# Transposed f16 adjacency parts made beside attention heads 3 to 7 instead of in a stage of their own

## The chip, the cores and the metric

The kernel runs on one NeuronCore of one Trainium2 chip. The metric is the device time of one execution in microseconds. Of the kernel before there are three timed runs (3369.71 to 3376.3, median 3375.74) and one profiled execution.

## The reference, cut to what matters

Four layers are computed on x (2048 nodes x 256) with one sparse adjacency matrix `adj` (2048 x 2048, f32). Each reads the layer-normed, rectified x and is added to x.

```
# layer 0: attention, 8 heads over all 2048 nodes
a = einsum('hnd,hmd->hnm', q, k) * scale + adj + adj       # entries with adj == 0 are masked
a = softmax(where(adj == 0, -1e6, a)); a = where(adj == 0, 0, a)
out = einsum('hnm,hmd->hnd', a, v) ... @ Wout
# layer 1: two steps, each with three products of 2048 x 2048 by 2048 x 256
S = adj + I; Rf = S / rowsum(S); Rb = S / colsum(S)[:, None]
Xf = Rf @ Xf; Xb = Rb @ Xb; Xa = nucleus(softmax(Q W2 K^T)) @ Xa
# layers 2 and 3: graph convolutions with adj and with adj + I, scaled by row sums
```

Layers 1 to 3 multiply by `adj` with the nodes on the contraction side, so the kernel keeps a transposed copy of 64·adj in device memory (`adjT_scratch`), as two f16 parts: a rounded one and the rest.

## The kernel before, in words

The kernel is a list of phases, with a barrier of all engines between them: `setup` (loads, layer norm, weights cut into f16 parts), `adjacency`, `attend` (layer 0), then layer 1 twice (`refresh`, `nucleus`), `onward` and `last`. Inside a phase each engine has its own program, in a written order, and waits on semaphores.

`adjacency` takes the 16 row tiles of adj (128 x 2048 f32, 1 MB each) through a ring of four buffers. The first four are loaded during `setup`; ScalarE issues the other loads (L385). Per tile, ScalarE copies it with its columns permuted (L373, which also makes the row sum). VectorE makes the attention bias from it (L405, L409), and SyncE stores the bias (1 MB, L339). TensorE transposes the 16 blocks of 128 x 128 into PSUM (L361), in two halves. For each half ScalarE writes the rounded f16 part (L378), and VectorE sums the columns (L413) and writes the rest part (L415). SyncE stores both parts (1 MB, L341).

`attend` runs 8 heads of 16 items; an item is 128 query rows against all 2048 keys. For item i:

- TensorE makes the logits: `qk`, 24 matmuls of 512 columns, L614, into two PSUM tiles `L` of two banks each.
- VectorE adds the bias and finds the maximum (`peaks`, two L759 of 1024 columns, then L768).
- ScalarE takes the exponential (`exp`: L682, L683) and writes its rounded f16 part e_hi (L688).
- VectorE writes the rest part e_lo (`lo`, L773) and the factors of the row (L776 to L779).
- SyncE's queue transposes both parts with DMA_TRANSPOSE, SBUF to SBUF (L495, L498), and loads the bias of item i+2 (L489).
- TensorE multiplies by V·Wout (`av`, 48 matmuls of 256 columns, L625), and VectorE adds the result to `acc` (`add`, L784).

The order of the engines in the loop of a head (14 turns, t = 0 to 13, with i = 16h + t) is written out: TensorE does qk(i+2), av(i). VectorE does lo(i+1), peaks(i+2), add(i), masks. ScalarE does exp(i+2). SyncE does the bias load and the two transposes of item i. In `exp` the write of e_hi waits for the transpose of the e_hi before it (one buffer), and `lo` for that of the e_lo before it.

At the turn of a head TensorE projects K, Q, V and V·Wout of the next head (`project`, L589 and L571); ScalarE and VectorE write each result bank as two f16 parts (`evacuate`, L695, L793). There are eight banks of PSUM: four in `L`, two `VP`, two `AVB`. The projection of K starts in the two `VP` banks (`EARLY = 2`) and then goes on in the four banks of `L`.

Of the kernel before, what the change touches and what calls it, by code (L numbers as in the profile page):

```python
# [31 lines left out]
ds = bass.ds  # L32

P = 128
# [72 lines left out]
def build(nc, a, out):  # L107
# [8 lines left out]
    with g:  # L116
# [31 lines left out]
        with ExitStack() as c:  # L148
# [4 lines left out]
            with ExitStack() as c1:  # L153
                rows = [sb(c1, f"adj_rows{u}", [P, N]) for u in range(ADJ_AHEAD)]
                phase(setup, a, bias_d, acc, ident, am, winv, sc, halfp, WH, WL, hT_hi, hT_lo, rows, rows_here)
                phase(adjacency, a["adj"], bias_d, at_d, sc, ident, deg, row_mask, rows, rows_here)
            phase(attend, a["L0_gnn_Wout"], bias_d, acc, ident, winv, sc, WH, WL, hT_hi, hT_lo, row_mask,
                  (a, deg, scales, ident16, halfp, gb, x_d, wtop))
# [152 lines left out]
def adjacency(nc, sb, ps, sem, adj, bias_d, at_d, sc, ident, deg, row_mask, A, loaded):  # L311
# [4 lines left out]
    (copied, zeroed, made, dve, tposed, hi_done, lo_done, summed) = (  # L316
        sem("adj_" + s) for s in ("copied", "zeroed", "made", "dve", "tposed", "hi", "lo", "summed"))
    stored = [sem(f"bias_stored{q}") for q in range(2)]
    at_stored = [sem(f"at_stored{q}") for q in range(2)]
    rows = adjacency_rows(adj)  # L320
    AHEAD = ADJ_AHEAD
    HALF = N // 2
    with ExitStack() as c:
        W = [sb(c, f"adj_permuted{q}", [P, N]) for q in range(2)]
        E = sb(c, "adj_zero", [P, N])
        count = sb(c, "adj_count", [P, T])
        B = [sb(c, f"adj_bias{q}", [P, N]) for q in range(2)]
        AT = [sb(c, f"adjT{q}", [P, 2, T, P], F16) for q in range(2)]
        col = sb(c, "col_parts", [P, T, T])
        TP = [ps(c, f"adj_tp{q}", [P, N]) for q in range(2)]  # L330
        FREE = 2
        block = nc.Block()
        with block:
            @block.sync
            def _(sp):
                def store(i, u):
                    n, q, turn = AHEAD * i + u, u % 2, 2 * i + u // 2
                    sp.wait_ge(made, n + 1 + FREE)
                    sp.dma_start(bias_d[ds(n, 1), :, :].rearrange("a p m -> p (a m)"), B[q][:, :]).then_inc(stored[q], 16)  # L339
                    sp.wait_ge(lo_done, 2 * n + 2 + 2 * FREE)  # L340
                    sp.dma_start(at_d[ds(n, 1), :, :].rearrange("a p m -> p (a m)"),  # L341
                                 AT[q][:, :, :, :].rearrange("p x m n -> p (x m n)")).then_inc(at_stored[q], 16)

                with sp.Fori(0, T // AHEAD) as i:
                    for u in range(AHEAD):
                        store(i, u)
                for q in range(2):
                    sp.wait_ge(stored[q], 16 * CH + 16)
                    sp.wait_ge(at_stored[q], 16 * CH + 16)

            @block.tensor
            def _(pe):
                with pe.Fori(0, T // AHEAD) as i:
                    for u in range(AHEAD):
                        n, q = AHEAD * i + u, u % 2
                        pe.wait_ge(loaded[u], 16 * i + 16)
                        rows_u = permuted(A[u][:, :])
                        for h in range(2):
                            pe.wait_ge(lo_done, 2 * n + h + 1)
                            for t in range(T // 2 * h, T // 2 * (h + 1)):  # L360
                                last = nc.tensor.transpose(TP[q][:, t * P:(t + 1) * P], rows_u[:, t // 2, t % 2 * P:(t % 2 + 1) * P], ident[:, :])  # L361
                            last.then_inc(tposed, 1)

            def half(x, h):
                return x[:, T // 2 * h:T // 2 * (h + 1), :].rearrange("p a b -> p (a b)")

            @block.scalar
            def _(s):
                def tile(i, u):
                    n, q, turn = AHEAD * i + u, u % 2, 2 * i + u // 2  # L370
# [4 lines left out]
                    s.wait_ge(at_stored[q], 16 * turn + 16)  # L375
                    for h in range(2):
                        s.wait_ge(tposed, 2 * n + h + 1)
                        nc.scalar.activation(half(AT[q][:, 0, :, :], h), TP[q][:, HALF * h:HALF * (h + 1)], ACT.Copy,  # L378
                                             scale=A_SCALE).then_inc(hi_done, 1)

                with s.Fori(0, T // AHEAD - 1) as i:
                    for u in range(AHEAD):
                        tile(i, u)
                        s.wait_ge(copied, AHEAD * i + u + 1)
                        s.dma_start(A[u][:, :], rows[ds(2 * i + 2 + u // 2, 1), u % 2, :, :].rearrange("a p m -> p (a m)")).then_inc(loaded[u], 16)  # L385
                for u in range(AHEAD):
                    tile(T // AHEAD - 1, u)

            @block.vector
            def _(v):  # L390
                nc.vector.memset(count[:, :], 0.0).then_inc(made, FREE)
                v.wait_ge(made, FREE)
                for q in range(2):
                    nc.vector.memset(count[:, :], 0.0).then_inc(stored[q], 16)
                    v.wait_ge(stored[q], 16)
                    nc.vector.memset(count[:, :], 0.0).then_inc(at_stored[q], 16)
                    v.wait_ge(at_stored[q], 16)
                nc.vector.memset(count[:, :], 0.0).then_inc(lo_done, 2 * FREE)
                v.wait_ge(lo_done, 2 * FREE)
                with v.Fori(0, T // AHEAD) as i:  # L400
                    for u in range(AHEAD):
                        n, q, turn = AHEAD * i + u, u % 2, 2 * i + u // 2
# [4 lines left out]
                        v.wait_ge(stored[q], 16 * turn + 16)  # L407
# [3 lines left out]
                        for h in range(2):  # L411
# [2048 lines left out]
```

## Time and profile before

| | |
|---|---|
| timed runs | 3369.71, 3375.74, 3376.3 us |
| profiled execution, its own time | 3375.48 us |
| its span | 3373.6 us |
| TensorE busy, weight loads | 2892.8 us (86%), 2147.8 us (64%) |
| VectorE, ScalarE busy | 2192.1 us (65%), 1342.0 us (40%) |
| granted TensorE clock, mean | 0.936 |
| DMA | 396.80 MB in 587856 packets, of which 538563 under 512 B |

A busy time is the union of an engine's instructions. Matmuls are pipelined and their ends are modelled, so a TensorE that shows as always busy can still have a little room. What paces a stretch is read from the order in time: which instruction each one starts behind. The span is divided by phases: `setup` up to 58 us, `adjacency` to 199 us, `attend` to about 1912 us, and layers 1 to 3 from there.

### The profile page before, as it was taken

How to read it: one execution, taken by the hardware profiler on the slowest of the kernel's cores; microseconds unless marked ns; L12 is line 12 of the kernel's file. 1: busy time of each engine (PE TensorE's matmuls, PEld its weight loads, DVE VectorE, ACT ScalarE, POOL GpSimd, SP SyncE). 2: the span in 40 equal slices, each digit the busy share in tenths (PEclk: the TensorE clock that was granted, in tenths of full speed). 3: DMA queues.
4: the chain of work that ended last, by engine and by line, in shares of the span. 5: the costliest groups of instructions: out<-in, count | busy, mean ns of one | idle time of the engine just before them, and what ended most of it. 6: DMA issues, size and time to landing. Idle time of an engine off the chain costs nothing. (4 is left out here: it accounts for less than half of the span.)

```text
span 3373.6 us, 55939 instructions
## 1 busy us (share of the span) xinstructions
PE 2892.8 (86%) x20376; PEld 2147.8 (64%) x20376; DVE 2192.1 (65%) x4346; ACT 1342.0 (40%) x1734; POOL 59.8 (2%) x71
## 2 busy tenths in 40 slices
PE   2469999999999999999999778878884669687599
PEld 1356676766767667676676447656553556576488
DVE  7966555565555655556556488788488887895531
ACT  5743434434344343443434322333326364522221
POOL 0000000000000000000000000000000000000110
PEclk7579999999999999999999889998997889899899
DMA  7937848578485784857848413000010010100500
GB/s 288 371 144 178 195 107 199 124 177 196 106 199 124 177 196 105 199 124 177 197 102 210 120 47 98 26 13 26 26 38 26 1 51 2 50 26 1 231 1 26
DMA packets 587856, 396.80 MB, mean 118 GB/s; under 512 B 538563, under 2 KB 553414, under 8 KB 562118
## 3 DMA queue, kind: packets, MB, share of 16 engines
q1 hardware_dynamic: 585990, 382.49, 42.1%
q10 hardware_dynamic: 1728, 12.58, 1.1%
q8 instruction: 72, 1.18, 0.2%
q14 instruction: 66, 0.54, 0.1%
HBM read 223.05 MB, written 37.75 MB: 77 GB/s over the span
## 5 line engine op out<-in xcount | busy, mean ns | idle before, releaser
L773 DVE SCALAR_TENSOR_TENSOR e_lo<-e,e_hi 128x2048 f16<-128x2048 f32 x128 | 293.2, 2291 | 435.3 <-ACT e_hi L688 435.3
L625 PE MATMUL av<-vw_hi,pT_hi 128*128 128x256 f16 x2048 | 559.5, 273 | 8.0 <-DMA pT_lo<-e_lo 8.0
L625 PE MATMUL av<-vw_hi,pT_lo 128*128 128x256 f16 x2048 | 559.4, 273 | 0.0
L625 PE MATMUL av<-vw_lo,pT_hi 128*128 128x256 f16 x2048 | 559.4, 273 | 0.0
L614 PE MATMUL logits<-kT_hi,qT_hi 128*128 128x512 f16 x1024 | 388.6, 379 | 2.8 <-DVE att_small L759 1.9
L614 PE MATMUL logits<-kT_lo,qT_hi 128*128 128x512 f16 x1024 | 388.1, 379 | 0.0
L614 PE MATMUL logits<-kT_hi,qT_lo 128*128 128x512 f16 x1024 | 388.1, 379 | 0.0
L682 ACT ACTIVATE att_small<-att_small,minus 128x1 f32<-128x1 f32 x128 | 37.6, 294 | 784.3 <-DVE att_small L768 784.3
L759 DVE CUSTOM_DVE_ANT_0 e<-logits,bias,att_small 128x1024 f32<-128x1024 f32 x256 | 328.6, 1283 | 0.4 <-issue 0.3
L2000 DVE SCALAR_TENSOR_TENSOR nuc_junk<-nuc_e,nuc_thr 128x2048 bf16<-128x2048 f32 x140 | 323.7, 2348 | 4.3 <-issue 0.4
L683 ACT ACTIVATE e<-e,att_small,sc 128x2048 f32<-128x2048 f32 x128 | 266.2, 2080 | 0.0
L688 ACT ACTIVATE e_hi<-e 128x2048 f16<-128x2048 f32 x128 | 244.5, 1910 | 15.2
L625 PEld LDWEIGHTS av<-vw_hi,pT_hi 128*128 128x128 f16 x2048 | 200.8, 98 | 44.7 <-issue 8.5
L625 PEld LDWEIGHTS av<-vw_lo,pT_hi 128*128 128x128 f16 x2048 | 200.8, 98 | 36.4
L625 PEld LDWEIGHTS av<-vw_hi,pT_lo 128*128 128x128 f16 x2048 | 200.8, 98 | 23.6
L1660 PE MATMUL nuc_l<-logit_k,logit_q 128*128 128x512 f32 x256 | 133.4, 672 | 62.0 <-ACT nuc_e L1855 56.0
L614 PEld LDWEIGHTS logits<-kT_hi,qT_hi 128*128 (+1 forms) x1024 | 100.0, 98 | 123.8 <-issue 15.8
L614 PEld LDWEIGHTS logits<-kT_hi,qT_lo 128*128 (+1 forms) x1024 | 100.2, 98 | 120.8
L614 PEld LDWEIGHTS logits<-kT_lo,qT_hi 128*128 (+1 forms) x1024 | 100.2, 98 | 106.4
L1636 PE MATMUL nuc_l<-nuc_u,nuc_xsT 128*128 128x256 f32 x320 | 92.4, 445 | 80.5 <-ACT nuc_xsT L1833 71.1
L361 PE MATMUL adj_tp<-ident,adj_rows 128*128 128x128 f32 x256 | 59.5, 411 | 91.4 <-DVE adjT L415 61.0
L1660 PEld LDWEIGHTS nuc_l<-logit_k,logit_q 128*128 128x128 f32 x256 | 53.3, 216 | 130.9 <-issue 65.8
(417 smaller groups left out, 5802.6 us busy)
## 6 DMA issues: line engine op xcount, KB each, us to landing
bias<-bias_scratch SPq DMA_DIRECT2D x130, 1024.0 KB, 4.9
bias_scratch<-adj_bias SPq DMA_DIRECT2D x16, 1024.0 KB, 4.5
adjT_scratch<-adjT SPq DMA_DIRECT2D x16, 1024.0 KB, 5.8
nuc_at_hi<-adjT_scratch SPq DMA_DIRECT2D x32, 512.0 KB, 3.8
nuc_at_lo<-adjT_scratch SPq DMA_DIRECT2D x32, 512.0 KB, 4.6
adjT<-adjT_scratch SPq DMA_DIRECT2D x16, 1024.0 KB, 19.8
adj_rows<-in_adj_dram ACTq DMA_DIRECT2D x12, 1024.0 KB, 6.8
adj_rows<-in_adj_dram SPq DMA_DIRECT2D x4, 1024.0 KB, 14.0
```

Of the source, the lines that this page charges most:

```text
L361: last = nc.tensor.transpose(TP[q][:, t * P:(t + 1) * P], rows_u[:, t // 2, t % 2 * P:(t % 2 + 1) * P], ident[:, :])
L614: last = nc.tensor.matmul(o, QT[w][:, k, ds(t * P, P)], KT[x][:, k, c0:c0 + BANK], start=(k == 0 and w == x == 0), stop=(k == 1 and w == 1))
L625: last = nc.tensor.matmul(AV[par], PT[par][w][:, m, :], VW[x][:, m, :], start=(m == 0 and w == x == 0), stop=(m == T - 1 and w == 1))
L682: nc.scalar.activation(masked(par), nb(par), ACT.Exp, bias=minus[:, 0:1], scale=1.0)
L683: nc.scalar.activation(E[par][:, :], E[par][:, :], ACT.Exp, bias=nb(par), scale=sc[:, 0:1], accum_out=ssum(par)).then_inc(exped, 1)
L688: nc.scalar.activation(EH[:, :], E[par][:, :], ACT.Copy, scale=P_SCALE).then_inc(hi_s, 1)
L759: return nc.vector.tensor_tensor_reduce(E[par][:, cols], L[half][:, :], B[par][:, cols], 1.0, (small[:, par, 6:7], m0(par))[half], ALU.add ...
L773: nc.vector.scalar_tensor_tensor(out=EL[:, :], in0=E[par][:, :], scalar=P_SCALE, in1=EH[:, :], op0=ALU.mult, op1=ALU.subtract).then_inc(lo ...
L1636: nc.tensor.matmul(WEIGHTED, xT[:, n * D + k * P:n * D + (k + 1) * P], U[:, n, k, :], start=(n == k == 0), stop=False)
L1660: last = nc.tensor.matmul(scores_in(i)[:, b * BANK:(b + 1) * BANK], QT[:, i * P:(i + 1) * P], KT[:, b * BANK:(b + 1) * BANK], start=True, ...
L2000: nc.vector.scalar_tensor_tensor(out=void[:, k % 2, :], in0=e[:, g % 2, k, 0:N], scalar=bound[:, k:k + 1], in1=e[:, g % 2, k, 0:N], op0=co ...
```

## The change

In `adjacency` the transposes, both f16 parts, their stores and the column sums by VectorE go. TensorE instead adds up the columns with a row of ones (64 f32 matmuls of 512 columns into one partition of PSUM), ScalarE copies the sums (one instruction over 1 x 2048), and 16 small matmuls turn them into columns. ScalarE issues the load that refills a buffer once its own copy and TensorE's sums have read it.

The transposed parts are made in `attend`, beside heads 3 to 7. The adjacency is read again from its input, in 64 pieces of 128 rows x 512 columns (256 KB). Heads 3 to 7 have 14 slots each, 70 in all, one per item of the loop; in slot s the engines do, with every step skipped where the piece doesn't exist:

- SyncE: first the four stores of piece s-3 (64 KB each, in runs of 128 f16 values), then item's bias load and two transposes, then the two DMA transposes of piece s-2 (128 x 512 each), then the load of piece s.
- ScalarE: after exp(i+2), the rounded part of piece s-1 (`piece_top`), read with its columns permuted.
- VectorE: after lo(i+1), peaks(i+2), add(i), masks (and, in head 7, shift), the rest part of piece s-1 (`piece_rest`), once ScalarE has made the top.

The pieces lie in columns of h^T that heads 0 to 3 have used up. The loops of heads 3 to 7 are written out on SyncE, ScalarE and VectorE. The projection of K goes over eight banks. In head 0 ScalarE evacuates V·Wout ahead of exp(0), and VectorE looks for the weights' maxima ahead of peaks(0).

```diff
 def adjacency(...)                                      # TensorE
+                    for b in range(N // BANK):
+                        cols = slice(b * BANK, (b + 1) * BANK)
+                        last = nc.tensor.matmul(CS[0:1, cols], ones[:, 0:1], A[n % AHEAD][:, cols], start=n == 0, stop=n == T - 1)
+                    last.then_inc(summed, 1)
...
                         s.wait_ge(copied, AHEAD * i + u + 1)
+                        s.wait_ge(summed, AHEAD * i + u + 1)
                         s.dma_start(A[u][:, :], rows[...]).then_inc(loaded[u], 16)
...
 def attend(...)
-        EARLY = 2
+        K_BANKS = (VP[0], VP[1], bank[2], bank[3], bank[0], bank[1], AVB[0], AVB[1])
...
+                def piece_load(n):                       # SyncE
+                    if n >= 2:
+                        sp.wait_ge(piece_lo, n - 1)
+                    sp.dma_start(PA[n % 2], piece_rows[tile // 2, tile % 2, part, :, :]).then_inc(piece_here[n % 2], 16)
+                def piece_turns(n):
+                    n -= 2
+                    sp.wait_ge(piece_lo, n + 1)
+                    if n:
+                        sp.wait_ge(piece_stored, 64 * n)
+                    for x in range(2):
+                        sp.dma_start_transpose(PX_T[x], PX[x]).then_inc(piece_turned, 16)
+                def piece_stores(n):
+                    n -= 3
+                    sp.wait_ge(piece_turned, 32 * n + 32)
+                    for x in range(2):
+                        for q in range(2):
+                            sp.dma_start(piece_out[tile, part % 2, :, x, :, q, part // 2, :],
+                                         PX_T[x][q * HALF:(q + 1) * HALF, :, :]).then_inc(piece_stored, 16)
+                def items_and_pieces(h):
+                    for t in range(T):
+                        piece_stores(slots(h, t))
+                        item(T * h + t, (t + 2) % T, t % 2)
+                        piece_turns(slots(h, t))
+                        piece_load(slots(h, t))
...
+                def piece_top(n):                        # ScalarE
+                    n -= 1
+                    s.wait_ge(piece_here[n % 2], 16 * (n // 2) + 16)
+                    if n:
+                        s.wait_ge(piece_turned, 32 * n)
+                    nc.scalar.activation(PX[0].rearrange("p (c r) -> p c r", c=CH), permuted(PA[n % 2]), ACT.Copy,
+                                         scale=A_SCALE).then_inc(piece_hi, 1)
+                def items_and_pieces(h):
+                    for t in range(SLOTS):
+                        exp(T * h + t + 2, t % 2)
+                        piece_top(slots(h, t))
...
+                def piece_rest(n):                       # VectorE
+                    n -= 1
+                    v.wait_ge(piece_hi, n + 1)
+                    nc.vector.scalar_tensor_tensor(out=PX[1].rearrange("p (c r) -> p c r", c=CH), in0=permuted(PA[n % 2]), scalar=A_SCALE,
+                                                   in1=PX[0].rearrange("p (c r) -> p c r", c=CH), op0=ALU.mult, op1=ALU.subtract).then_inc(piece_lo, 1)
+                def items_and_pieces(h):
+                    for t in range(SLOTS):
+                        item(h, t, t % 2, link)          # lo(i+1), peaks(i+2), add(i), masks
+                        if h == HEADS - 1:
+                            shift(T * h + t, t, t % 2)
+                        piece_rest(slots(h, t))
```

## Rows read from the trace of the kernel before

**Rows 1.** Windows: busy us and count per engine, granted clock, DMA share, GB/s

```profile
core 0: us, PE busy (x) PEld busy (x) DVE busy (x) ACT busy (x) POOL busy (x), PEclk, DMA share, GB/s
64.00:164.00 100.00, 46.82 (x202) 37.78 (x200) 97.58 (x85) 71.03 (x50) 0.00 (x0) 0.59 0.98 373
205.00:1860.00 1655.00, 1639.44 (x11967) 1165.46 (x11966) 964.86 (x1908) 683.31 (x759) 8.19 (x3) 1.00 0.66 160
```

**Rows 2.** Timelines of VectorE and ScalarE over one item: start, duration, [idle before]

```profile
912.38 2.29 DVE L773 SCALAR_TENSOR_TENSOR e_lo<-e,e_hi 128x2048 f16<-128x2048 f32 x1 [3.94 <-ACT e_hi L688]
915.29 1.28 DVE L759 CUSTOM_DVE_ANT_0 e<-logits,bias,att_small 128x1024 f32<-128x1024 f32 x1
918.11 0.21 DVE L768 TENSOR_SCALAR att_small<-att_small,sc 128x1 f32<-128x1 f32 x1
918.36 0.29 ACT L682 ACTIVATE att_small<-att_small,minus 128x1 f32<-128x1 f32 x1 [6.12 <-DVE att_small L768]
920.85 1.91 ACT L688 ACTIVATE e_hi<-e 128x2048 f16<-128x2048 f32 x1
922.91 2.29 DVE L773 SCALAR_TENSOR_TENSOR e_lo<-e,e_hi 128x2048 f16<-128x2048 f32 x1 [3.91 <-ACT e_hi L688]
```

**Rows 3.** Timeline of TensorE: the first logits matmul of two items

```profile
927.85 0.38 PE L614 MATMUL logits<-kT_hi,qT_hi 128*128 128x512 f16 x1
938.27 0.38 PE L614 MATMUL logits<-kT_hi,qT_hi 128*128 128x512 f16 x1
```

**Rows 4.** Instruction groups: what copies and rests of this shape took

```profile
L373 ACT ACTIVATE adj_permuted<-adj_rows x16: 3913/3944/4097, 58.2 to 175.3; 128x2048 f32<-128x2048 f32 x16
L706 ACT ACTIVATE wo_hi<-wo_stage,winv x8: 705/706/722, 203.2 to 1682.1; 128x512 f16<-128x512 f32 x8
L805 DVE SCALAR_TENSOR_TENSOR wo_lo<-wo_stage,winv,wo_hi x8: 750/751/753, 204.0 to 1682.9; 128x512 f16<-128x512 f32 x8
```

**Rows 5.** Timeline of SyncE's queue over one item: issue start and length

```profile
912.35 1.72 SPq L495 DMA_TRANSPOSE pT_hi<-e_hi  x1
914.77 2.17 SPq L498 DMA_TRANSPOSE pT_lo<-e_lo  x1
918.27 0.33 SPq L489 DMA_DIRECT2D bias<-bias_scratch  x1
922.87 1.92 SPq L495 DMA_TRANSPOSE pT_hi<-e_hi  x1
1761.09 1.05 SPq L515 DMA_DIRECT2D x_scratch<-wo_stage  x1
```

**Rows 6.** DMA: one item, a transposing microsecond, a bias microsecond; packets and issues

```profile
912.35:922.87 10.52, 10.52 (x76) 7.14 (x74) 6.28 (x13) 4.28 (x4) 0.00 (x0) 1.00 0.84 199
916.00:917.00 1.00, 1.00 (x12) 0.89 (x10) 0.88 (x4) 0.00 (x0) 0.00 (x0) 1.00 1.17 224
910.00:911.00 1.00, 1.00 (x6) 0.49 (x5) 0.00 (x0) 0.87 (x3) 0.00 (x0) 1.00 1.02 434
DMA packets 4317, 2.10 MB, mean 191 GB/s; under 512 B 4189, under 2 KB 4189, under 8 KB 4189
pT_lo<-e_lo SPq DMA_TRANSPOSE x128, 4.3
```

**Rows 7.** Adjacency: VectorE's groups, the last stores, a later f32 matmul

```profile
L405 DVE TENSOR_SCALAR adj_zero<-adj_permuted x16: 1212/1216/1228, 62.5 to 185.9; 128x2048 f32<-128x2048 f32 x16
L409 DVE SCALAR_TENSOR_TENSOR adj_bias<-adj_permuted,sc,adj_zero x16: 2351/2352/2353, 63.9 to 187.2; 128x2048 f32<-128x2048 f32 x16
194.29 0.33 SPq L341 DMA_DIRECT2D adjT_scratch<-adjT  x1
199.23 0.39 SPq L537 DMA_DIRECT2D wo_stage<-in_L_gnn_Wout_dram  x1
bias_scratch<-adj_bias SPq DMA_DIRECT2D x16, 1024.0 KB, 4.5
2841.31 3.70 PE L1660 MATMUL nuc_l<-logit_k,logit_q 128*128 128x512 f32 x8
```

**Rows 8.** Waits of TensorE, 205 to 1860 us: total, times, longest

```profile
PE logits L589 <- DVE kT_lo L793: 9.4, 7, 1.4
PE vw_ps L571 <- DVE vw_lo L793: 3.4, 1, 3.4
```

More of the change, by code:

```diff
@@ L326, in adjacency @@
         count = sb(c, "adj_count", [P, T])
+        ones = sb(c, "adj_ones", [P, 1])
         B = [sb(c, f"adj_bias{q}", [P, N]) for q in range(2)]
[L328 to L330 removed]
+        col = sb(c, "col_sums", [1, N])
+        CS = ps(c, "col_sums_ps", [P, N])
+        CT = ps(c, "col_sums_turned", [P, BANK])
         FREE = 2
@@ L351, in _ @@
             @block.tensor
             def _(pe):
[L353 to L362, printed above, removed]
@@ L367, in _ @@
+                pe.wait_ge(row_here, 1)
+                for t in range(T):
+                    last = nc.tensor.matmul(CT[:, t:t + 1], permuted(col[0:1, :])[:, t // 2, t % 2 * P:(t % 2 + 1) * P], ones[0:1, 0:1],
+                                            start=True, stop=True)
+                last.then_inc(turned, 1)
             @block.scalar
@@ L395, in _ @@
                     v.wait_ge(stored[q], 16)
[L396 to L402, printed above, removed]
+                with v.Fori(0, T // 2) as i:
+                    for q in range(2):
+                        n = 2 * i + q
                         v.wait_ge(copied, n + 1)
@@ L470, in attend, with piece, slots @@
         AV = [AVB[n][:, 0:D] for n in range(2)]
-        EARLY = 2
+        bank = [L[b // 2][:, b % 2 * BANK:(b % 2 + 1) * BANK] for b in range(4)]
         VW_RING = (VP[0], VP[1], AVB[0])
+        K_BANKS = (VP[0], VP[1], bank[2], bank[3], bank[0], bank[1], AVB[0], AVB[1])
         GAMMA_BETA_READ = 9
-        bank = [L[b // 2][:, b % 2 * BANK:(b % 2 + 1) * BANK] for b in range(4)]
         kinds = [(1, KT), (0, QT), (2, VT), None]
+        done_h = [[hT[:, k, 0:(FIRST_HEAD + 1) * ROWS] for k in range(KC)] for hT in (hT_hi, hT_lo)]
+        PA = [done_h[0][k].bitcast(F32) for k in range(KC)]
+        PX = [done_h[1][0][:, x * BANK:(x + 1) * BANK] for x in range(2)]
+        PX_T = [done_h[1][1][:, x * BANK:(x + 1) * BANK].rearrange("p (b n) -> p b n", n=P) for x in range(2)]
+        def piece(n):
+            tile, part = n // PARTS, n % PARTS
+            return tile, part
+        def slots(h, t):
+            return SLOTS * (h - FIRST_HEAD) + t if isinstance(h, int) and h >= FIRST_HEAD and t < SLOTS else None
         def m0(par): return small[:, par, 0:1]
@@ L708, in begin @@
                         evacuate(h, n)
-                    exp(T * h, 0)
-                    evacuate(h, 3)
+                    if isinstance(h, int) and h == 0:
+                        evacuate(h, 3)
+                        exp(T * h, 0)
+                    else:
+                        exp(T * h, 0)
+                        evacuate(h, 3)
                     exp(T * h + 1, 1)
@@ L902, in _ @@
                     masks(2, 0, link)
-                link = items(HEADS - 1, ends=True)
+                with v.Fori(0, FIRST_HEAD) as h:
+                    turn_of_heads(h, items(h))
+                for h in range(FIRST_HEAD, HEADS - 1):
+                    turn_of_heads(h, items_and_pieces(h))
+                link = items_and_pieces(HEADS - 1)
                 lo(T * HEADS - 1, 1, link)
```

141 lines of the change are left out of this document (80 added, 61 removed).

## The prediction

> **What bounds the kernel now.** I read the windows by stage first. In the adjacency stage VectorE is busy 97.58 of 100 us and the DMA engines show a share of 0.98 at 373 GB/s [rows 1]: two limits at once. In the attention stage TensorE is busy 1639 of 1655 us at full clock, and VectorE and ScalarE only 58% and 41% [rows 1]. Read alone, this says that VectorE and ScalarE have time to spare there. So I read next, in time order, what starts behind what over one item of a head [rows 2]. The reader is to see one closed chain:
>
> - VectorE's e_lo starts at 912.38, the moment e_hi is there; the logits' maxima follow without a gap (first half at 915.29), and the factor of L768 starts at 918.11.
> - ScalarE starts at 918.36, ends e_hi at 920.85 + 1.91 = 922.76, and VectorE's next e_lo starts at 922.91.
>
> Nobody outside of the chain is waited for. VectorE's idle 3.94 us is ScalarE's part of it, ScalarE's idle 6.12 us is VectorE's. The chain takes 922.91 - 912.38 = 10.53 us per item. TensorE's own work takes 938.27 - 927.85 = 10.42 us per item [rows 3]. So two loops run with nearly the same period, and in neither engine of the chain is the idle time free: whatever stands inside it lengthens the item, whatever stands beside it does not.
>
> **The pieces, beside heads 3 to 7.** In slot t ScalarE runs exp(i+2) and then `piece_top`. VectorE runs lo(i+1), peaks(i+2), add(i), masks, and then `piece_rest`, which waits for the top of the same slot, so for the whole of exp(i+2). Behind the waiting instruction in VectorE's queue stands lo(i+2), which before started right at e_hi(i+2). Everything the piece costs on both engines is therefore put into the chain between e_hi and e_lo:
>
> - `piece_top`, 128 x 512 f32 read with permuted columns (a step of 8 values). The same permuted copy of four times the size took 3944 ns, while the contiguous e_hi of that size took 1.91 us [rows 2, 4]. A contiguous 128 x 512 copy took 706 ns [rows 4]. With a fixed part of about 0.3 us (from 0.706 and 1.91 us on a straight line), the permuted one is 0.3 + (3.94 - 0.3)/4 = 1.2 us. Bounds: 0.7 (contiguous) and 1.35 us.
> - `piece_rest`, the same shape on VectorE: 0.75 us contiguous [rows 4]. No permuted read by VectorE is in the trace. I take 0.75, because the nearest row is of the same operation and size. Upper bound: 0.75 x 3.94/1.91 = 1.5 us.
> - One more handover between the engines, 922.91 - 922.76 = 0.15 us [rows 2].
>
> Sum 2.1 us, bounds 1.55 and 3.0. The item of a slot becomes 10.53 + 2.1 = 12.6 us. There are 64 pieces in 64 slots: 64 x 2.1 = **+134 us** (99 to 192). TensorE then idles 12.6 - 10.4 = 2.2 us per item. The trace has whole attention windows at clock 1.00 only with TensorE nearly full; I take 1.00 also here and put its fall into the upper part of the range.
>
> The Trainium skill's page "SBUF — State Buffer", section "Door 1: The DMA port swizzle", says that an SBUF access leaves full bandwidth once successive reads fall into new 16-byte lines, that is at a step above 4 f32 values. ScalarE's 3944 ns agree with it. By this rule VectorE's permuted read would be slowed too, which is the third rival below.
>
> **The DMA queue in a slot.** An item moves two transposes and one bias load. A transposing microsecond moves 224 GB/s at a share of 1.17, a bias microsecond 434 GB/s [rows 6]. So the 1 MB of the transposes takes 4.8 us and the 1 MB of the bias 2.4 us, with start-up gaps a share of 0.84 [rows 6]. A piece adds transposes of 0.25 MB (1.2 us), a load of 0.25 MB (0.6 us), and 0.25 MB of stores in 1024 runs of 256 B. No store of such runs is in the trace. The transposes' packets are 256 B too (1.05 MB in 4096 of the 4189 small ones), so I take their rate, 1.2 us; bounds 0.6 (the bias rate) and 2.6 us (twice the transposes' time). Together 4.8 + 2.4 + 1.2 + 0.6 + 1.2 = 10.2 us, which fits in 12.6 but would hardly have fitted in 10.5.
>
> SyncE's queue is in order, so I followed it, from e_hi at 0. The transpose of e_hi is issued at 0.1. The e_lo transpose is issued at 4.5 (e_lo is 2.1 late), its issue takes 2.2 and it lands 4.3 later [rows 5, 6]. The piece's transposes are issued behind it, about 0.5 us each, and land at 10.0. The load's issue may take 1.05 us, as the store behind a transpose did [rows 5]. The stores wait for that landing: issued from 10.05 to 11.4, and the bias load behind them at 11.4 instead of right behind the maxima. The next e_hi transpose comes at 12.7 and finds the bias still moving, up to 15. It ends near 17.4, before the e_lo transpose would start at 18.3. So the next e_lo is not late, and av(i), which needs it, runs from 11.6 while both have landed by 8.9. Cost 0, thanks to the chain having grown. The margin is about 1 us; what it costs without it is rival 2.
>
> The Trainium skill's page "DMA: Bandwidth & Descriptors", section "Specifications", asks for at least 512 B per run for line rate and calls smaller ones read-modify-write. The stores here are 256 B; no run of before shows such a store.
>
> **The adjacency stage.** Of VectorE's 8.2 us per tile (15 steps from 63.9 to 187.2) there remain L405 and L409, 1.22 + 2.35 + about 0.35 = 3.9 us [rows 7]. ScalarE keeps the copy, 3.94 + 0.2, and an issue, about 4.6 us. TensorE's four f32 matmuls per tile take 4 x 0.44 = 1.8 us at full clock (3.70 us for eight [rows 7]) and twice that at half clock; both lie below ScalarE. The new wait for `summed` holds only ScalarE's reload behind it, and TensorE is ahead. DMA: before, 12 loads and 32 stores of 1.05 MB; now 12 and 16, 29.4 MB. At 373 to 380 GB/s this is 78 us, above ScalarE's 16 x 4.6 = 74. From the first reload at 63.0 it ends at 141, and 3 us go on the last landing: 144. Before, the last store was issued at 194.3 and the next phase issued at 199.2 [rows 7]; the last of the new stores lands where I put 144 to 146. The column sums' tail (copy of 1 x 2048 about 2 us, 16 small matmuls about 2) lies beside the last bias (2.35 us and 4.5 us to land [rows 7]). Saved: **-53 us** (bounds -40, if the DMA falls to 320 GB/s in so mixed a traffic, and -58, if ScalarE sets the pace).
>
> **The turn of heads and head 0.** K over eight banks takes away the wait for the first K rest, 9.4 us in 7 turns [rows 8]. In the three turns before the pieces it is gone: -4. In the four turns beside pieces the K evacuation starts 2 us later and the gain is used up by it: 0 (-5 to +7). In head 0 TensorE's 3.4 us wait goes: **-3** (0 to -3.4). Layers 1 to 3 read the same bytes from the same place: 0.
>
> **Sum.** The profiled execution's own time 3375.5 (span 3373.6 and 1.9 around it; the median is 3375.7, so nothing is to be shifted): 3375.5 - 53 - 4 - 3 + 134 = 3449.5. I predict 3448 us. About 0.2% (7 us) can be told from no change.
>
> **Rivals.**
>
> 1. Faster: the pieces are free, because they fit in VectorE's 3.9 and ScalarE's 6.1 us of idle time per item. For it: the busy shares of 58% and 41%. Against it: these gaps wait for each other and for nothing else. It decides if e_lo doesn't have to follow e_hi at once, from a slack of 2.1 us per item. Then 3375.5 - 53 - 9 - 3 = 3310 us.
> 2. The DMA queue sets the item. If each 256 B store costs 2.6 us or its four issues take 0.9 us each (one took 1.05 behind a transpose), the loop from stores over bias, e_hi, e_lo and piece transposes back to the stores is 0.7 + 3.6 + 2.7 + 4.8 + 1.2 + 0.6 = 13.6 us, with a slow bias start 14. Then 64 x (13.9 - 10.5) = 218: 3375.5 - 60 + 218 = 3533 us.
> 3. VectorE's permuted read is slowed as ScalarE's is. For it: ScalarE's 3.94 against 1.91 us [rows 2, 4]. Against it: nothing measured. The rest then takes 1.35 to 1.5 us: + 64 x 0.6 to 0.75, so 3490 us.
> 4. The pieces come out at half their price, since the DVE and ScalarE parts overlap in their pipelines or TensorE's loop had been the longer one in the first half of a head: 64 x 1.1: 3386 us.
>
> Chances: forecast 0.53, rival 1 0.09, rival 2 0.13, rival 3 0.18, rival 4 0.07. Range 3396 to 3520: it holds the forecast with its bounds, rival 3, and the lower part of rival 2, and leaves out rival 1, most of rival 4 and the rest of rival 2. Faster 0.11 (rival 1, and a little of rival 4), within 0.2% 0.03, slower 0.86.
>
> **What the profile after would show.** The e_lo group has a start to start of 12.6 us in slots against 10.5 in heads 0 to 2; `piece_top` near 1.2 us, `piece_rest` near 0.75; between e_hi and e_lo about 2.2 us instead of 0.15; ScalarE's idle before L682 still near 6, now ended by the same L768; TensorE with a gap of 2 us per item; the first item of attention starting near 147 instead of 202. If the e_lo instructions stay 10.5 us apart, rival 1 holds. If ScalarE waits for `hi_turned` or TensorE for pT_lo, it is rival 2. The forecast fails altogether if the order of `piece_rest` and the next `lo` turns out not to bind.

## The result and the profile after

| | median us | runs | ratio to before, 95% interval |
|---|---|---|---|
| before | 3372.72 | 3365.39 to 3376.3 (4) | |
| after | 3788.04 | 3781.08 to 3792.01 (4) | 1.1231, 1.1207 to 1.1254 |

The change makes the kernel 415 us slower. The prediction was 3448 us with a range to 3520: the sign was right, the size of the loss was not. The profiled execution took 3786.7 us (span 3784.9).

First where the time went. The three lines are VectorE's e_lo instructions (count, duration min/median/max in ns, first to last start in us) in before, in after, and in the first experiment, which has no pieces:

```profile
L773 DVE SCALAR_TENSOR_TENSOR e_lo<-e,e_hi x128: 2279/2292/2294, 258.6 to 1894.1; 128x2048 f16<-128x2048 f32 x128
```

```profile
L839 DVE SCALAR_TENSOR_TENSOR e_lo<-e,e_hi x128: 2276/2286/2295, 208.9 to 2312.6; 128x2048 f16<-128x2048 f32 x128
```

```profile
L845 DVE SCALAR_TENSOR_TENSOR e_lo<-e,e_hi x128: 2280/2292/2293, 214.6 to 1832.2; 128x2048 f16<-128x2048 f32 x128
```

The first e_lo comes 258.6 - 208.9 = 49.7 us earlier. Most of it is the adjacency stage: attention's first load is issued at 152.04 for 199.23 [rows 7], 47.2 us earlier, where 53 were forecast. From the first e_lo to the last it takes 2103.7 us for 1635.5, +468. Behind the last one are 3784.9 - 2312.6 = 1472.3 us for 1479.5, -7. Sum -49.7 + 468.2 - 7.2 = +411, the difference of the two spans. The loss lies in the heads with pieces alone: from the first e_lo of head 0 to that of head 3 it takes 627.1 us for 629.0, from there to the last e_lo 1476.6 for 1006.5.

The windows of after, to be read against [rows 1]: VectorE falls from 97.58 to 63.88 us and the DMA share from 0.98 to 0.85 in the adjacency stage; in attention TensorE is idle 244 of 1655 us and its granted clock is 0.92 for 1.00. Over this window no engine is near full, and the DMA engines' share is 0.65 (0.70 in items with pieces, see run 16).

```profile
core 0: us, PE busy (x) PEld busy (x) DVE busy (x) ACT busy (x) POOL busy (x), PEclk, DMA share, GB/s
64.00:164.00 100.00, 76.60 (x235) 26.59 (x233) 63.88 (x79) 66.36 (x38) 4.00 (x2) 0.86 0.85 326
205.00:1860.00 1655.00, 1410.79 (x9613) 977.79 (x9612) 811.11 (x1577) 597.97 (x653) 0.00 (x0) 0.92 0.65 150
```

So one item has to be read in order of time, as [rows 2] and [rows 5] were. SyncE's queue in one slot of after (issue start and length), then ScalarE, then VectorE (start, duration, [idle before]):

```profile
1303.76 0.60 SPq L487 DMA_DIRECT2D bias<-bias_scratch  x1
1304.50 5.45 SPq L493 DMA_TRANSPOSE pT_hi<-e_hi  x1
1310.07 1.87 SPq L496 DMA_TRANSPOSE pT_lo<-e_lo  x1
1316.14 2.50 SPq L516 DMA_TRANSPOSE hT_lo<-hT_lo  x2
1318.69 0.57 SPq L506 DMA_DIRECT2D hT_hi<-in_adj_dram  x1
1319.86 2.58 SPq L526 DMA_DIRECT2D adjT_scratch<-hT_lo  x4
1322.48 0.61 SPq L487 DMA_DIRECT2D bias<-bias_scratch  x1
1323.23 5.41 SPq L493 DMA_TRANSPOSE pT_hi<-e_hi  x1
```

```profile
1312.07 1.91 ACT L732 ACTIVATE e_hi<-e 128x2048 f16<-128x2048 f32 x1 [6.63 <-DMA pT_hi<-e_hi]
1313.89 1.11 ACT L773 ACTIVATE hT_lo<-hT_hi 128x512 f16<-128x512 f32 x1
1321.81 0.30 ACT L726 ACTIVATE att_small<-att_small,minus 128x1 f32<-128x1 f32 x1 [6.82 <-DVE att_small L834]
1330.87 1.91 ACT L732 ACTIVATE e_hi<-e 128x2048 f16<-128x2048 f32 x1 [6.67 <-DMA pT_hi<-e_hi]
```

```profile
1315.03 1.08 DVE L929 SCALAR_TENSOR_TENSOR hT_lo<-hT_hi,hT_lo 128x512 f16<-128x512 f32 x1 [10.70 <-ACT hT_lo L773]
1316.02 2.29 DVE L839 SCALAR_TENSOR_TENSOR e_lo<-e,e_hi 128x2048 f16<-128x2048 f32 x1
```

The item takes 1330.87 - 1312.07 = 18.80 us for 10.53, and it is one loop that now runs through SyncE's queue. From e_hi's start: e_hi to the top 1.82 us, top to rest 1.14, rest to the issue of the piece's transposes 1.11; then SyncE alone: transposes 2.55, load with the wait for the transposes' landing 1.17, four stores 2.62, bias load 0.75; and at 1323.23 the transpose of the e_hi that was written at 1312.07. It was ready 9.2 us earlier (at 1312.07 + 1.91). It takes 5.4 us to issue, and ScalarE's next e_hi starts 7.64 us behind its start. Sum 1.82 + 1.14 + 1.11 + 2.55 + 1.17 + 2.62 + 0.75 + 7.64 = 18.80. The next item's exponential was ready at 1324.1 already; ScalarE then waits for the transpose to land, because there is one buffer for e_hi.

The same in the waits of after (engine, line, what for: total us, times, longest), SyncE's own among them:

```profile
DVE hT_lo L929 <- ACT hT_lo L773: 651.5, 64, 11.9
ACT e_hi L732 <- DMA pT_hi<-e_hi: 374.9, 60, 7.0
PE av L670 <- DMA pT_lo<-e_lo: 339.6, 57, 7.9
SPq L516 <- DVE hT_lo L929: 259.6, 60, 7.6
```

The first line tempts: VectorE waits 651 us for `piece_top`. But the top is a late link of the loop, not its price; the price is in what stands between e_hi and its transpose.

### The profile page after: what moved, and what is told of

It reads as the page before. It is cut to its first block and busy times, and to the rows that moved or that the text cites. A ratio compares the mean times of both kernels' runs of the same rounds, so it can differ in the third digit from the quotient of the medians.

```text
span 3784.9 us, 54717 instructions
## 1 busy us (share of the span) xinstructions
PE 3028.1 (80%) x20280; PEld 2174.1 (57%) x20280; DVE 2173.5 (57%) x4344; ACT 1380.7 (36%) x1767; POOL 57.8 (2%) x71
## 5 line engine op out<-in xcount | busy, mean ns | idle before, releaser
L670 PE MATMUL av<-vw_hi,pT_hi 128*128 128x256 f16 x2048 | 615.5, 301 | 339.6 <-DMA pT_lo<-e_lo 339.6
L670 PE MATMUL av<-vw_lo,pT_hi 128*128 128x256 f16 x2048 | 614.8, 300 | 0.0
L670 PE MATMUL av<-vw_hi,pT_lo 128*128 128x256 f16 x2048 | 612.4, 299 | 0.0
L670 PEld LDWEIGHTS av<-vw_hi,pT_hi 128*128 128x128 f16 x2048 | 219.8, 107 | 415.7 <-issue 365.9
L929 DVE SCALAR_TENSOR_TENSOR hT_lo<-hT_hi,hT_lo 128x512 f16<-128x512 f32 x64 | 69.0, 1078 | 651.5 <-ACT hT_lo L773 651.5
L732 ACT ACTIVATE e_hi<-e 128x2048 f16<-128x2048 f32 x128 | 244.7, 1912 | 381.3 <-DMA pT_hi<-e_hi 374.9
L670 PEld LDWEIGHTS av<-vw_lo,pT_hi 128*128 128x128 f16 x2048 | 219.1, 107 | 49.2
L670 PEld LDWEIGHTS av<-vw_hi,pT_lo 128*128 128x128 f16 x2048 | 220.5, 108 | 45.0
```

Of the source, the lines that this page charges most:

```text
L670: last = nc.tensor.matmul(AV[par], PT[par][w][:, m, :], VW[x][:, m, :], start=(m == 0 and w == x == 0), stop=(m == T - 1 and w == 1))
L732: nc.scalar.activation(EH[:, :], E[par][:, :], ACT.Copy, scale=P_SCALE).then_inc(hi_s, 1)
L929: nc.vector.scalar_tensor_tensor(out=PX[1].rearrange("p (c r) -> p c r", c=CH), in0=permuted(PA[n % 2]), scalar=A_SCALE, in1=PX[0].rearran ...
```

## The experiments

"Slot" is the time of an item with a piece. "Issue" of a DMA is the time that it holds SyncE's queue, and "landing" the moment when its data are there. All times are medians; the kernel before ran beside each set (3370.2 to 3374.3 us).

**1. No pieces.** `PIECES = 0`; the scratch gets the same 16 MB in sixteen 1 MB stores of weights, so the transposed adjacency is missing from it.

```diff
-    PIECES = T * PARTS
+    PIECES = 0
+                        sp.dma_start(at_d[n // 4, :, :], WH[0][...]).then_inc(filled, 16)     # n % 4 == 0
```

> The kernel after with no pieces at all: no loads, tops, rests, transposes or stores of pieces; the transposed parts are not made (16 stores of 1 MB of weights, one in every fourth item of heads 3 to 6, fill the scratch instead). All that is left of the change is the shorter adjacency stage, K over eight banks and the order in head 0. Theory A (SyncE's in-order queue closes a loop through the pieces) and theory B (the DMA engines are full of the 256 B stores) both expect the terms of the prediction without the pieces: 3375 - 53 - 9 - 3 = 3310 us, 3306 to 3325. A third theory, that something else in the change costs (the loops written out, the layers behind), expects 3340 us or more.

3308.39 us, ratio 0.9809 (0.9793 to 0.9826). The sum of all terms but the pieces' was right: in the prediction it was 3375.5 - 60 = 3315. The pieces cost 3788.0 - 3308.4 = 480 us, forecast 134.

The sum, 62 us less than the kernel before where 60 were forecast, is right partly by luck. In this run's trace the first e_lo comes at 214.6, 44 us earlier than before, so the first part saved less than forecast. And from the first e_lo of head 3 to the last it takes 991.0 us, for 1001.7 in run 17, which has the same turn of heads and no pieces either, but loops that are not written out. These 11 us stand in no term of the prediction; they fit the written-out loops (or another order of waits in them), which no run tried alone.

**2. Loads, tops and rests only** (transposes and stores of pieces out, fills in).

```diff
 def piece_turns(n):
+    return
 def piece_stores(n):
+    return
```

> Pieces are loaded, and ScalarE's top and VectorE's rest are made where the change has them; no transposes and no stores of pieces (the parts in the scratch are those of e1). This is the term of +134 us in the prediction by itself. After it, the top takes 1.11 and the rest 1.08 us in the trace of the changed kernel, so the chain should be 10.53 + 1.11 + 1.08 + 0.15 = 12.9 us per slot: e1 + 64 x 2.3 = e1 + 150 us, about 3460. Both theories expect this. If VectorE and ScalarE had time to spare after all, it is e1 + 0 to 30.

3474.98 us: +166.6, 2.6 us a slot. SyncE's wait before the load (for the rest of two pieces earlier, 252.4 us in all) already puts load, bias and pT_hi's transpose behind the next e_hi, and the long issue is here already. So this run is not the chain's +134 alone:

```profile
1396.88 0.33 SPq L507 DMA_DIRECT2D hT_hi<-in_adj_dram  x1
1397.26 0.43 SPq L488 DMA_DIRECT2D bias<-bias_scratch  x1
1397.81 5.06 SPq L494 DMA_TRANSPOSE pT_hi<-e_hi  x1
```

**3. Everything but the stores.**

> As the change, but without the stores of the pieces (their place in the scratch is filled as in e1); loads, tops, rests and the pieces' transposes stand where they were. Theory A: SyncE still waits in slot s for a rest that comes only behind the NEXT e_hi, then issues 2.5 us of transposes, 0.6 of load, 0.6 of bias before that e_hi's transpose. Loop: 0.15 + 1.1 + 1.1 + 2.5 + 0.6 + 0.6 + landing 5 to 6 + 1.9 = 13 to 14 us, e1 + 64 x 3.0 = e1 + 160 to 220. Theory B: without the stores the DMA engines are no limit, and it equals e2.

3644.53 us: +169.6 over run 2, 2.65 us a slot, which is the issue of the two transposes (2.50 us and a gap). The last step, the stores, gives 3788.0 - 3644.5 = 143.5, 2.24 us a slot, for an issue of 2.58, against which run 3 has a quarter of a fill a slot (0.43/4 us). Both of the expected sizes were wrong: in this order, every issue on SyncE counts nearly in full.

**4. Another order on SyncE:** bias, pT_hi, the piece's transposes (one slot later), pT_lo, load, stores.

```diff
-                        piece_stores(slots(h, t))
-                        item(T * h + t, (t + 2) % T, t % 2)
-                        piece_turns(slots(h, t))
-                        piece_load(slots(h, t))
+                        item(..., between=lambda: piece_turns(s_ - 1))      # between pT_hi and pT_lo
+                        piece_load(s_ - 1)
+                        piece_stores(s_)
```

> All work of the change, but SyncE's order moved: in a slot it issues bias, transpose of e_hi, the two transposes of a piece whose rest is due by then (one slot later than in the change), transpose of e_lo, load, stores. Tops and rests stay in the chain. Theory A: the wait for a rest behind the next e_hi is gone, SyncE's issues add up to 10.3 us, and the slot falls from 18.8 to 13 to 14.5 us: 3450 to 3580 us. Theory B (the DMA engines need 18 us for a slot's bytes): within 30 us of the changed kernel, 3760 or more.

3534.33 us, ratio 1.048 (1.0459 to 1.0502): 254 us come back with the same work. SyncE's wait for the rest is gone (259.6 us before, 0.3 us here), and its queue is now full, with no pause:

```profile
1397.54 5.31 SPq L493 DMA_TRANSPOSE pT_hi<-e_hi  x1
1402.95 2.51 SPq L517 DMA_TRANSPOSE hT_lo<-hT_lo  x2
1405.58 1.46 SPq L497 DMA_TRANSPOSE pT_lo<-e_lo  x1
1407.10 1.31 SPq L507 DMA_DIRECT2D hT_hi<-in_adj_dram  x1
1408.45 2.58 SPq L527 DMA_DIRECT2D adjT_scratch<-hT_lo  x4
1411.08 0.61 SPq L487 DMA_DIRECT2D bias<-bias_scratch  x1
1411.83 5.39 SPq L493 DMA_TRANSPOSE pT_hi<-e_hi  x1
```

The slot of 1411.83 - 1397.54 = 14.3 us is the sum of its issues, 13.8 us, and the gaps between them.

**5. `piece_top` ahead of `exp`**, one line moved.

> One line moved: ScalarE makes the top of a piece before exp(i+2), in the time in which it waits for VectorE, instead of behind it. So the rest no longer stands between e_hi and e_lo, and it is made before the next e_hi, where SyncE asks for it. All work of the change is done. Theory A (loop and issue time of SyncE's queue): the loop through the rest opens, and what is left is the sum of SyncE's issues in a slot, as in e4: 1.9 + 2.5 + 0.6 + 0.6 + 2.6 + 0.6 + 5.3 = 14.1 us against 10.3: e1 + 64 x 3.8 to 4.5, 3550 to 3600. The theory that only VectorE's and ScalarE's 2.3 us count: changed kernel - 150 = 3640.

3564.51 us, ratio 1.0557 (1.054 to 1.0575). The rest is there when SyncE asks for it: its wait falls from 259.6 to 9.0 us in all, and the item (e_hi at 1397.63 and 1412.42) takes 14.8 us, near the sum of SyncE's issues as in run 4.

**6. Stores in runs of 1 KB** instead of 256 B: another order of the blocks in the scratch, and later stages take them in it.

```diff
-    piece_out = at_d.rearrange("t (h r) (x b a q n) -> t h r x b a q n", ...)
+    piece_out = at_d.rearrange("t (h r) (x a q b n) -> t h r x b a q n", ...)
```

> Only the layout of the scratch changes: the four blocks of a piece lie side by side, so a store moves runs of 1 KB instead of 256 B (64 runs per store instead of 256), and the consumers index the blocks in the new order. Theory A: a store's issue falls from 0.62 to 0.35 us (-1.1 per slot), and the bias load and e_hi's transpose behind it start earlier by the time that the 1024 small runs needed, 3 to 4 us in the trace of the change: 18.8 to about 14 us, 3788 - 64 x 4.5 = 3500, range 3480 to 3620. If the runs' size is without effect on the DMA engines: -64 x 1.1, 3718.

3788.96 us, ratio 1.1235 (1.1216 to 1.1253): no difference, with 684903 packets for 734055. Both expected sizes fell. The four stores' issue is hardly shorter (2.38 us for 2.58), so the queue has as much to issue as before, and what the wider runs save on the DMA engines is hidden.

**7. Piece loads and stores issued by GpSimd.**

> The loads and the stores of the pieces are issued by GpSimd, which is idle, instead of SyncE; SyncE keeps bias, transposes of e and of pieces in the change's order, and with it the wait for a rest behind the next e_hi. Same bytes, same small runs. Theory A: it is e3 without the load's issue on SyncE: 3590 to 3660. Theory B (the 256 B stores fill the DMA engines): the stores are still there, so no gain: 3750 or more.

3674.85 us, ratio 1.0893 (1.0875 to 1.0912): 113 us less, and 15 us above theory A's range. SyncE still waits 271.3 us for the rest.

**8. Runs 5, 6 and 7 together, the piece's transposes behind the next bias load.**

> All repairs together: top before exp, runs of 1 KB, loads and stores of pieces issued by GpSimd, and on SyncE the piece's transposes behind the next item's bias load, so the bias is not directly ahead of e_hi's transpose. SyncE's issues sum to 0.4 + 2.5 + 1.9 + 2.0 = 6.8 us per slot, the DMA engines' bytes to 9.8 us, both below 10.5. Theory A: all is hidden, e1 + 0 to 60, 3310 to 3370, below the kernel before. If DMAs issued by GpSimd or the traffic as such delay the transposes: 3400 or more.

3412.11 us, ratio 1.0109 (1.0092 to 1.0126). This missed the expected range: 104 us over run 1 are left.

**9. The bias load issued by ScalarE**, behind its e_hi, and nothing else.

```diff
 # SyncE, item
-                    sp.wait_ge(logits_read, 2 * i + 2 + READS_FREE)
-                    bias(after, par)
 # ScalarE, exp
                     nc.scalar.activation(EH[:, :], E[par][:, :], ACT.Copy, scale=P_SCALE).then_inc(hi_s, 1)
+                    s.dma_start(B[par][:, :], bias_d[ds(after, 1), :, :]...).then_inc(bias_par[par], 16)
```

> The change as it is, but each bias load is issued by ScalarE, right behind its e_hi write, and no longer by SyncE directly ahead of pT_hi's transpose. Theory A (a transposing DMA that stands directly behind a load in SyncE's queue holds SyncE until that load has landed: its issue takes 5.4 us for 1.9): the slot loses 0.6 us of the bias issue and 3 to 3.5 us of pT_hi's issue, 64 times: 3790 less 230 to 265 us, 3525 to 3560. Theory B (the long issue comes of the DMA engines being shared with the bias load, whoever issues it): the issue stays near 5 us, 3740 to 3790. Theory C (the piece loads and stores behind it in the queue fill the gap): stores now stand directly ahead of pT_hi, and its issue stays above 4 us, 3680 to 3750.

3582.58 us, ratio 1.063 (1.0612 to 1.0648): 205 us less, 3.2 a slot, 23 us above theory A's range and far from the two others. pT_hi's transpose, now behind four stores and not behind the bias load, is issued in 2.0 us:

```profile
1396.99 2.58 SPq L526 DMA_DIRECT2D adjT_scratch<-hT_lo  x4
1399.69 1.96 SPq L493 DMA_TRANSPOSE pT_hi<-e_hi  x1
```

The run moved the load to another queue and to another time at once. ScalarE issues it at 1404.25, and the next transpose of e_hi comes at 1414.89, when the load (median landing 5.3 us) is there. So it shows that the load just ahead was the cause, but it does not decide between theories A and B, because the load was no longer moving. Sorted by this, the transposes of e_hi from 900 us on took 1.96 us (median of 58) where the load had landed and 3.35 us (median of 17) where it was still moving, though in ScalarE's queue; directly behind the load in SyncE's queue they take 5.3.

**10. Run 8's early top, wide stores and GpSimd, with the bias load on ScalarE.**

> SyncE issues transposes only: loads and stores of the pieces are issued by GpSimd, bias loads by ScalarE behind its e_hi write, and piece_top comes before the exp that waits for pT_hi. Theory A (the loss is SyncE's serial issue and its waits): SyncE's sum per slot is 2.5 + 1.9 + 1.9 = 6.3 us for about 12 us of a slot, all hidden; 3308 (the run without pieces) to 3350 us. Theory B (the DMA queues' own time: the extra transposing moves, 0.5 MB a slot at 200 GB/s, 2.5 us, in a row with the tiles' own): 2 to 3 us a slot stay, 3430 to 3500.

3435.62 us, ratio 1.0187 (1.017 to 1.0204). Theory A fell, and the time is in theory B's range. In the slots of head 5 SyncE issues for 8.1 us of 12.5, and the slot stays near 12. Before the piece's transposes SyncE waits for the landing of the stores, 180.6 us in all.

**11. Early top, and loads and stores by GpSimd; SyncE in the change's order.**

> The change with its piece loads and stores issued by GpSimd and piece_top ahead of the exp; SyncE keeps piece transposes, bias, pT_hi, pT_lo in the change's order. Theory A: SyncE issues 2.5 + 0.6 + 5.4 + 1.9 = 10.4 us a slot, and the loop from the rest of a piece to its transposes no longer passes the exp: 3320 to 3420 us. Theory B (early top does not help once the stores have left SyncE; the loop stays e_hi write, rest, turns, bias, pT_hi): near the 3675 us that the queue move alone gave, 3600 to 3680.

3409.77 us, ratio 1.0112 (1.0095 to 1.0129). The slot is the sum of SyncE's issues, 2.50 + 0.57 + 5.09 + 3.15 and gaps, 11.8 us (piece transposes to piece transposes, 1421.67 - 1409.87). The issue of pT_lo is longer here than in after (3.15 us for 1.87), so an issue is not a fixed price:

```profile
1409.87 2.50 SPq L516 DMA_TRANSPOSE hT_lo<-hT_lo  x2
1412.42 0.57 SPq L487 DMA_DIRECT2D bias<-bias_scratch  x1
1413.13 5.09 SPq L493 DMA_TRANSPOSE pT_hi<-e_hi  x1
1418.34 3.15 SPq L496 DMA_TRANSPOSE pT_lo<-e_lo  x1
1421.67 2.50 SPq L516 DMA_TRANSPOSE hT_lo<-hT_lo  x2
```

**12. Early top and bias on ScalarE, the rest as in the change.**

> piece_top ahead of the exp and bias loads issued by ScalarE; loads and stores of the pieces stay with SyncE. Theory A: the two savings add where they take different parts of the loop: the early top gave 224 us and the bias 230 to 265 us of 412 above the kernel before; SyncE's sum is 2.5 + 0.6 + 2.6 + 1.9 + 1.9 = 9.5 us, below a slot of 11.7, so what is left is small: 3320 to 3400 us. Theory B (the issue of pT_hi stays long with four stores directly ahead of it): SyncE's sum is 13 us a slot, 3400 to 3480.

3537.64 us, ratio 1.05 (1.0483 to 1.0518), a miss, and only 27 us below run 5. With the long issue gone SyncE comes early to the stores and stands before them until the piece's transposes have landed, 193.1 us in all for 33.6 in run 5. Early top and bias on ScalarE shorten the same loop and hardly add.

**13, 14. Halves with semaphores of their own** on runs 8 and 10 (a half's transpose waits only for that half's two stores). These runs have 256 B stores again, which runs 8 and 10 had not: two differences at once.

```diff
                     for x in range(2):
+                        if n:
+                            sp.wait_ge(piece_stored[x], 32 * n)
-                        sp.dma_start_transpose(PX_T[x], PX[x]).then_inc(piece_turned, 16)
+                        sp.dma_start_transpose(PX_T[x], PX[x]).then_inc(piece_turned[x], 16)
```

> Piece loads and stores issued by GpSimd, piece_top ahead of the exp, a piece's transposes behind the next bias load, and each half of a piece with semaphores of its own: the transpose of a half waits for that half's two stores alone, and the stores for that half's transpose alone. Theory A (the loop through the turned buffer: transposes issued and landed 5.2 us, stores issued and landed 6.9 us, 12.2 us a slot, set e8_pool_all's 3412): the loop of one half is about 4 + 1 + 4 + 1.3 us = 10.5, below the item's own 10.5 to 11, so 3310 to 3360. Theory B (the DMA engines are the bound, 0.95 of 12.3 us = 11.7 us of work a slot): at least 3308 + 64 x 0.8 = 3360, and hardly below e8: 3370 to 3415.

> The same split halves with bias loads issued by ScalarE, transposes alone with SyncE. Theory A: e10_act_bias_all's loop of 11.9 us and more falls to about 10.5: 3310 to 3360. Theory B (DMA engines at 0.94 busy): 3390 to 3436, as e10.

3411.67 us (1.0118, 1.0095 to 1.0141) and 3437.19 us (1.0208, 1.0176 to 1.0241): as runs 8 and 10, and within theory B's range or 1 us above it.

**15. Run 13 with stores in runs of 1 KB.**

> e13_split_order with its stores in runs of 1 KB for 256 B (layout of the scratch and the order in which later stages take its tiles changed with it). Theory A (packets of 256 B fill the DMA engines, which are now the bound, as they were not when e6_wide_runs changed nothing): 50,000 packets fewer, 3350 to 3390 us. Theory B (the store's packets are no more than a small part of what fills them): 3405 to 3415, as e13.

3388.57 us, ratio 1.0044 (1.0027 to 1.006). Against run 13 the wide runs give 23.1 us; against run 8, which has wide runs and whole-piece semaphores, the split gives 23.5 us. Run 13 alone reads as if the split changed nothing, and so I first read it; it had lost as much by its narrow runs. The fourth combination, narrow runs and no split in this order, was not run.

**16. Run 13 without the stores** (fills as in run 1).

> e13_split_order without the 256 piece stores; the same 16 MB go to the scratch as sixteen fills of 1 MB from weights (so the transposed adjacency is not in it). Loads, tops, rests and piece transposes stay. Theory A (the DMA engines are full and the stores' packets are a part of it): the slot falls to the item's own, 3310 to 3345 us. Theory B (the piece transposes fill them, or hold up the tiles' own transposes whatever is stored): 3380 to 3412.

3328.05 us, ratio 0.9874 (0.9852 to 0.9896). Of the 103 us that run 13 stands over run 1, 84 are the stores and the loop through them; 20 us are left for loads, tops, rests and transposes.

How full are the DMA engines? A window has to be cut by items: with a turn of heads in it, where they have less to do, the share comes out lower. So here are the same eight items (from the sixth e_hi of head 5 to the fourteenth) of run 1, after, run 13, run 15 and run 16:

```profile
1311.11:1392.30 81.19, 81.19 (x567) 55.28 (x566) 48.93 (x102) 34.27 (x33) 0.00 (x0) 1.00 0.93 233
```

```profile
1532.67:1681.34 148.67, 102.38 (x576) 64.12 (x576) 57.17 (x112) 42.41 (x40) 0.00 (x0) 0.82 0.70 155
```

```profile
1351.95:1450.84 98.89, 88.23 (x581) 57.81 (x579) 57.19 (x112) 42.70 (x41) 24.47 (x40) 0.97 1.16 233
```

```profile
1340.78:1435.80 95.02, 85.47 (x582) 56.31 (x581) 56.74 (x112) 43.19 (x41) 22.05 (x41) 1.00 1.16 244
```

```profile
1318.92:1405.51 86.59, 84.85 (x581) 56.44 (x579) 57.24 (x112) 42.81 (x40) 4.29 (x8) 1.00 1.11 267
```

Item times share gives the DMA work of an item: 10.15 x 0.93 = 9.4 us in run 1, 18.6 x 0.70 = 13.0 in after, 12.4 x 1.16 = 14.3 in run 13, 10.8 x 1.11 = 12.0 in run 16. A piece thus adds 3.6 us (after) to 4.9 us (run 13) to the work of run 1's item. A share of 1 is no limit of this measure (it reaches 1.16 here, and 1.17 in [rows 6]), but in run 13 it is as high as anywhere, at 233 GB/s where a bias load alone moved 434 [rows 6].

With SyncE relieved (run 10), the limit is therefore on the DMA side. Two things can make it: the work as such, or the loop of a piece (transposes landed, stores landed, next transposes), in which each landing is late while others move. Run 15 shortened the work and gained 23 us; run 16 took away work and loop at once. They are not told apart.

**17. K over eight banks alone**, on the kernel before (with head 0's new order), five rounds.

> The kernel before with K over eight banks, and head 0's order of exp and V W_o evacuation as in the change; adjacency stage and attention queues as before. Theory A (the run without pieces, 62 us below the kernel before, is the sum of 50 us of the adjacency stage and some 12 us of this part): 3355 to 3365 us. Theory B (the 12 us came of the removed adjacency work, for instance of its later loads, and K's banks gain nothing): 3368 to 3373.

3364.48 us (3360.43 to 3367.39), ratio 0.9974 (0.9963 to 0.9984). This is the only complete kernel here that is faster than the one before, by 8.1 us or 0.24%; the prediction had given these edits 7.

## Why the prediction was off

- **Adjacency stage** (-53 forecast): 47.2 us in after; by the first e_lo, which includes head 0's new order, 49.7 in after and 44.0 in run 1. **Turn of heads and head 0** (-7): 8.1 us in run 17. **Layers 1 to 3** (0): -7 us in the spans of after and before, within the spread of the kernel before (3365.39 to 3376.3). These steps held in kind, with the adjacency stage 6 to 12 us too high; run 1's sum agrees because heads 3 to 7 gave 11 us that no term had.
- **`piece_top`** (1.2 us): 1.11. **`piece_rest`** (0.75, with rival 3 at 1.35 to 1.5): 1.08. VectorE's permuted read is slowed, though less than rival 3 says. As in the Trainium skill's "SBUF — State Buffer", Door 1, the trace agrees that a step of 8 f32 values costs bandwidth on VectorE too. This explains 0.33 x 64 = 21 us of the 346 by which the pieces were under-priced.
- **The failed step** is the DMA queue in a slot, "Cost 0, thanks to the chain having grown". It says that "the piece's transposes are issued behind" the e_lo transpose, at about 7 us behind e_hi, and takes the piece's rest as there. But these transposes are of piece s-2, whose rest VectorE makes in its slot s-1, behind ScalarE's exp and top of that slot, so behind e_hi(i+1). SyncE takes its queue in order: at its wait for that rest (259.6 us, 60 times) it stops, and the transposes, the load, the stores and the bias load all come between e_hi(i+1) and its own transpose. I followed the queue, but did not write down which slot makes the thing each wait asks for. Run 4 shows it: the same instructions in another order, -254 us. The sign that the prediction gave for rival 2 is there: ScalarE waits for e_hi's transpose (374.9 us), TensorE for pT_lo (339.6 us).
- **Mis-sized terms of the same step:** the piece's transposes 0.5 us each to issue (1.26 measured), the four stores 1.35 us in all (2.58), and the transpose of e_hi, which finds the bias still moving, 4.7 us from issue to landing (12.7 to 17.4; 7.6 us measured, 5.4 of them in the issue). Taking the bias load away from there is worth 3.2 us a slot (run 9). Rival 2 had the right kind, an item set by the queue, but a loop of 13.9 us for 18.8, for the same reason.
- **The sum of DMA work**, 10.2 us for item and piece, was 13.0 in after. Its first part was against a row already: it has 7.2 us for the item, and [rows 6] gives 0.84 x 10.5 = 8.8. In the change's order this cost nothing, since the queue was the longer one; once the queue was mended it is what is left over.
- **The stores' run length** was the worry that both the trace (256 B packets) and the Trainium skill's "DMA: Bandwidth & Descriptors", Specifications (at least 512 B for line rate), gave. It cost nothing while the queue was the bound (run 6) and 23 us once the limit was on the DMA side (run 15 against 13).
- **Rival 1** (pieces free in the engines' idle time) is close to run 16: 20 us for everything but stores, once tops are early. The bound "whatever stands inside the chain lengthens the item" was right for the change's order, and an order without it existed.

What stays open: on the DMA side, work or loop (run 16). And why SyncE's issue is long behind the bias load. That it lasts until this load has landed fits closely: in all 56 such issues of after from 900 us on, it ended 0.08 to 0.30 us before the landing. But a transpose takes longer also while a load of another queue moves (3.35 us, run 9) or GpSimd's stores do (3.15 us for pT_lo, run 11), so the place in the queue is only part of it. No run had the same load at the same time in another queue.

## What to carry to other kernels

Before putting work "beside" a loop, write for each wait of an in-order queue in which turn its producer runs, and list everything queued behind it until the loop's own next instruction: where this closes a loop, that sum, issues included, is the item's time, whatever the busy shares say. A cheap order of issue (a piece's transposes one turn later, its first step ahead of the long wait) was worth 224 to 254 us here; who issues a load, and with it when, 205. When one bound is lifted the next hides the worth of further edits, so test two of them in all four combinations.

## What was not expected of the hardware

- A DMA transpose of 128 x 2048 f16 issued right behind a 1 MB load in the same queue (0.14 us after the load's issue ended) holds the queue 4.9 to 5.6 us (median 5.28 of 56 in after; 5.38 of 58 in run 11). Behind four 64 KB stores it took 2.0 us (run 9), and 1.7 to 1.9 us where the load was issued more than 4 us earlier [rows 5].
- The issue of the same transpose is longer while other transfers move: pT_lo took 1.87 us in after and 3.15 in run 11, where GpSimd's stores ran beside it.
- Issue costs on SyncE: 1.26 us for a transpose of 128 x 512, 0.62 us for a 64 KB store of 256 B runs, 0.57 us for a 256 KB load (1.31 directly behind a transpose, run 4).
- With transposes of f16 and short stores in the mix, the DMA engines show a share of 1.16 over eight items at only 233 GB/s (run 13); the bias load alone moved 434 at 1.02 [rows 6].
- A permuted read (step of 8 f32) of 128 x 512 took 1.08 us on VectorE for 0.75 contiguous, and 1.11 on ScalarE for 0.71 [rows 4].
